# An attention and expert kernel: the start-up of the attention phase in another order, and two tensor-engine waits at other places in every pass

## The reference

```python
xn = layernorm(x)
# attention on xn, 16 heads of 64, latent width 128
h = layernorm(xn) * ln_scale + ln_bias
c_q, c_kv = h @ w_down_q.T, h @ w_down_kv.T
q, k, v = c_q @ w_up_q.T, c_kv @ w_up_k.T, c_kv @ w_up_v.T     # then rotary turns on q and k
s = softmax(q k^T / 8) v @ w_out.T + xn
# mixture of 8 experts on xn, the two best per token, each with a capacity
g = silu(experts(xn) + xn)
out = x + s * g
```

## Time and profile before

| | |
|---|---|
| median of 3 runs | 3656.07 us (3655.32 to 3656.79) |
| the profiled execution | 3655.32 us, its span 3653.8 us |
| PE busy | 3599.4 us, 99% of the span |
| DVE busy | 3195.1 us, 87% |
| ACT busy | 2759.1 us, 76% |
| POOL busy | 1199.8 us, 33% |
| granted TensorE clock | 0.998 of full speed over the span |

### The profile page before, as it was taken

How to read it: one execution, slowest core, us unless ns; L and a number is a source line. 1 busy time by engine, 2 the same in 40 slices (tenths; PEclk the granted TensorE clock), 3 DMA queues, 4 the chain that set the end, 5 groups by cost and what they waited for, 6 DMA issues and landing times. The chain is left out here.

```text
span 3653.8 us, 77190 instructions
## 1 busy us (share of the span) xinstructions
PE 3599.4 (99%) x24217; PEld 2364.0 (65%) x24217; DVE 3195.1 (87%) x4341; ACT 2759.1 (76%) x4016; POOL 1199.8 (33%) x1178
## 2 busy tenths in 40 slices
PE   7999999999999999999999999999999999999999
PEld 5754554545544554545554555454699999999999
DVE  8889999999999999999999999999777777777799
ACT  5778888888878888888888888888766666666665
POOL 2212222222222222222222222232366666666400
PEclk9999999999999999999999999999999999999999
DMA  7985767676666666666667676765666666666798
GB/s 257 358 283 142 185 156 186 157 185 161 180 160 176 170 174 169 171 171 166 177 165 181 160 186 156 184 162 136 193 222 215 217 223 216 214 224 216 235 369 274
DMA packets 378436, 724.74 MB, mean 198 GB/s; under 512 B 105277, under 2 KB 253886, under 8 KB 342272
## 3 DMA queue, kind: packets, MB, share of 16 engines
q0 software_dynamic: 83504, 340.66, 36.2%
q1 hardware_dynamic: 294864, 383.23, 31.8%
HBM read 453.60 MB, written 138.81 MB: 162 GB/s over the span
## 5 line engine op out<-in xcount | busy, mean ns | idle before, releaser
L1180 ACT ACTIVATE at_ex<-at_st 128x1024 f32<-128x1024 f32 x1024 | 1048.8, 1025 | 138.3 <-PE at_st L1327 132.8
L1383 PE MATMUL at_pv<-at_ex,at_v 128*64 128x512 f32 x4096 | 991.6, 605 | 0.0
L1037 DVE TENSOR_REDUCE at_mx<-at_fr 128x1 fp32r<-128x512 f32 x1024 | 705.9, 689 | 202.5 <-PE at_fr L1393 169.6
L1204 ACT ACTIVATE at_fr<-at_fr 128x512 f32<-128x512 f32 x1024 | 603.4, 589 | 243.0 <-PE at_fr L1393 229.7
L1383 PEld LDWEIGHTS at_pv<-at_ex,at_v 128*64 128x64 f32 x4096 | 248.3, 136 | 471.1 <-issue 462.2
L1050 DVE TENSOR_TENSOR at_sum<-at_sum,at_ex 128x1024 f32<-128x1024 f32 x448 | 545.3, 1217 | 3.7 <-ACT at_ex L1180 3.4
L1393 PE MATMUL at_fr<-at_kfar,at_qh 64*128 64x512 f32 x1024 | 459.7, 449 | 5.9 <-DVE at_mx L1037 4.5
L1390 PE MATMUL at_fr<-at_kdif,at_qh 64*128 64x512 f32 x1024 | 461.4, 451 | 1.8 <-DVE at_mx L1037 0.9
L1327 PE MATMUL at_st<-at_qh,at_kh 64*128 64x512 f32 x2048 | 452.8, 392 | 3.8 <-DMA at_top<-at_mneg 3.7
L1390 PEld LDWEIGHTS at_fr<-at_kdif,at_qh 64*128 64x128 f32 x1024 | 187.7, 183 | 413.7 <-issue 356.9
L1327 PE MATMUL at_st<-at_ql,at_kh 64*128 64x512 f32 x2048 | 452.0, 391 | 0.0
(11 more groups left out here) (213 smaller groups left out, 6359.4 us busy)
## 6 DMA issues: line engine op xcount, KB each, us to landing
at_cq<-scr_c SPq DMA_DIRECT2D x62, 1024.0 KB, 6.1
at_ck<-scr_c SPq DMA_DIRECT2D x62, 1024.0 KB, 5.2
at_sum<-at_sum POOLq DMA_DIRECT2D x95, 512.0 KB, 6.0
scr_v<-pj_v SPq DMA_DIRECT2D x64, 512.0 KB, 6.8
at_v<-scr_v SPq DMA_DIRECT2D x64, 512.0 KB, 6.6
mid_rec<-scr_rec SPq DMA_DIRECT2D x256, 128.0 KB, 5.1
scr_o<-mid_oT SPq DMA_DIRECT2D x64, 512.0 KB, 3.0
at_rotq<-at_swpq POOLq DMA_DIRECT2D x126, 256.0 KB, 4.6
```

The lines of the kernel that those rows point to most:

```text
L1037: e.reduce_max(mx[k // QB][:, h * QB + k % QB:h * QB + k % QB + 1], fr[h][:, :], AX.X).then_inc(s_tr[h], 1)
L1180: e.activation(ex[k][:, :, :], st[u % 2][:, :, :], ACT.Exp, scale=SCALE).then_inc(s_exp, 1)
L1204: e.activation(fr[h][:, :], fr[h][:, :], ACT.Relu).then_inc(s_pos[h], 1)
L1383: mm = e.matmul(pv[n][rows[h], :], v[i.u][:, kt, rows[h]], ex[kt][:, h, :], start=(kt == 0), stop=(kt == KT - 1))
```

## The change

It has four pieces.

1. **SP's prologue.** The loads of pair 2's weights (`load_w(At(0, 2), x)`) and the move of the first maxima go from behind the second value store to behind all value stores, behind the wait for their completion, and behind `load_v` of pair 0.
2. **PE's prologue and the routing.** The second routing product goes to the other half of `st[0]` in place of `pv[0]`. All four routing matmul groups are issued at k = 3 and 4, the two projections of pair 2 after them, the second one after k = 5. PE now waits for the rank ahead of body 0, where it waited for the totals. DVE does one more piece of `choice` (three, not two) before body 0. ACT's copies follow the projections.
3. **ACT's bodies.** Copies of the second projection halves (`proj_copy(two, K, 1)` and `proj_copy(three, Q, 1)`) move from the beginning of steps 4 and 0 to the end of the step before.
4. **PE's bodies.** `side_ready(g)`, which matters at g = 1 and g = 4, moves from behind `scores(2g+1)` to between `scores(2g)` and `scores(2g+1)`. A wait of `side(4)` for a copy joins it.

```diff
-        route_at = [st[0][:, 0, :], pv[0][:, :]]
+        route_at = [st[0][:, n, :] for n in range(2)]
...
                     if t == 1:
                         pj_compressed()
-                        e.wait_ge(s_made, 4)
-                        for x in (Q, K):
-                            e.wait_ge(s_pr, projected(At(0, 0), x, 1))
-                            load_w(At(0, 2), x)
-                            e.sem_inc(s_ld[x][0], 16)
-                e.wait_ge(s_init, 2)
-                max_rows(At(0, 0), 0)
                 pj["stored"](e)
                 pj["values_stored"](e)
                 load_v(At(0, 0))
+                for x in (Q, K):
+                    e.wait_ge(s_pr, projected(At(0, 0), x, 1))
+                    load_w(At(0, 2), x)
+                    e.sem_inc(s_ld[x][0], 16)
+                e.wait_ge(s_init, 2)
+                max_rows(At(0, 0), 0)
...
-                for _ in range(2):
+                for _ in range(3):
                     next(choice)
...
-                    if g == 0 and prev and ahead >= 2:
-                        proj_copy(two, Q, 1, pv[0])
-                    if g == 4 and ahead >= 2:
-                        proj_copy(two, K, 1, pv[1])
...
-                    if g == 1 and ahead >= 2:
-                        proj_copy(two, K, 0, pv[1])
+                    if g in (1, 3) and ahead >= 2:
+                        proj_copy(two, K, g // 2, pv[1])
...
-                    if g == 5 and ahead >= 3:
-                        proj_copy(three, Q, 0, pv[0])
+                    if g in (5, 7) and ahead >= 3:
+                        proj_copy(three, Q, (g - 5) // 2, pv[0])
...
-                    if k == 3:
-                        e.wait_ge(s_raw[K], 4)
-                        project(third, Q, 0, pv[1])
+                    if k in (3, 4):
+                        next(choice)
                     if k == 4:
-                        next(choice)
                         e.wait_ge(s_raw[K], 3)
                         e.wait_ge(s_init, 3)
                         turn_maxima(first, 0)
-                    if k == 5:
-                        e.wait_ge(s_neg, 1)
-                        next(choice)
                     step_y(first, k)
...
-                    if k == 3:
+                    if k in (3, 4):
                         next(choice)
                     if k == 4:
-                        e.wait_ge(s_raw[Q], 5)
-                        project(third, Q, 1, pv[1])
-                    if k == 5:
-                        next(choice)
+                        e.wait_ge(s_raw[K], 4)
+                        project(third, Q, 0, pv[1])
+                e.wait_ge(s_raw[Q], 5)
+                project(third, Q, 1, pv[1])
                 e.wait_ge(s_init, 2)
-                rt["counted"](e)
+                rt["ranked"](e)
...
                         scores(i, 2 * g)
+                        side_ready(g)
                         scores(i, 2 * g + 1)
-                    side_ready(g)
```

More of the change, by code:

```diff
@@ L704, in vector @@
             e.tensor_scalar(keep["widx"][:, :], who[:, :], float(P), part[:, 0:1], ALU.mult, ALU.add).then_inc(s_done, 1)
-        def counted(e):
-            e.wait_ge(s_v, 1)
         def ranked(e):
@@ L716, in done @@
             e.wait_ge(s_done, 3)
-        return {"vector": vector, "scalar": scalar, "tensor": tensor, "counted": counted, "ranked": ranked, "spread": spread, "done": done}
+        return {"vector": vector, "scalar": scalar, "tensor": tensor, "ranked": ranked, "spread": spread, "done": done}
 def attend_parts(nc, ctx, below, bridge, io, scr, keep, pj, rt):
@@ L1248, in prologue @@
                     if k == 4:
-                        proj_copy(third, Q, 0, pv[1])
                         negate(first, 0)
                     if k == 5:
-                        proj_copy(third, Q, 1, pv[1])
+                        proj_copy(third, Q, 0, pv[1])
                     gain(first, k, 1, s_y)
@@ L1257, in prologue @@
                         pj_value(2 * k + 3)
+                proj_copy(third, Q, 1, pv[1])
                 pj["values_stored"](e)
@@ L1512, in bank_free @@
                         e.wait_ge(s_neg, i.n(2, 1))
-                        if not prev:
-                            rt["ranked"](e)
                     elif prev:
@@ L1538, in side_ready @@
                             e.wait_ge(s_one[n], prev.n(16, 16))
+                        if ahead >= 2:
+                            e.wait_ge(s_raw[K], two.n(2, 2))
+                        else:
+                            e.wait_ge(s_neg, i.n(2, 2))
                 def side(g):
@@ L1550, in side @@
                     if g == 4 and prev:
[L1551 to L1554, removed]
                         denominators(prev)
```

## The result

The changed kernel takes 3683.36 us (median of 4, 3681.42 to 3687.47), the kernel before 3656.43 us (median of 4): 1.0075 times the time before, 95% interval 1.0057 to 1.0092. I had forecast 3680 us, 1.0065. A repetition in another session gave 3682.45 us, 1.0062 (1.0045 to 1.0079) of a kernel before that took 3660.38 there.

The account below looks back on a forecast made before the run. PE, busy 2098.21 of 2100 us, bounds the steady bodies; DVE paces body 0. Span 3653.8 + 12.8 (bodies) + 11.0 (prologue) = 3677.6, with 1.5 around it 3679.1, median 0.75 higher: 3680 us; 8-in-10 range 3667 to 3690.

Parts of the forecast that it names:

- The g = 1 wait: PE's bodies: `scores(3)` waits for ACT's copy, net 0.21 us in each of 61 bodies, 12.8 us in all.
- The wait at g = 4: PE's bodies, before `scores(9)`: its additions and copy come while PE still has four score pairs; cost taken as nothing.
- `step_y`'s own small stall: PE's step 1: 0.11 us against an undisturbed start, expected to disappear because `gain` is by then long over.
- ACT's copies at zero: ACT's bodies: the moved copies, about 0.6 us each, fit barely into gaps before steps 4 and 0; no cost.
- The prologue: Parts 1 and 2: 10.5 for later body 0, 1.7 for the clock, 1.2 back: +11.0 us, bounds +6 to +17.
- The landing of the weights: SP's prologue: pair 2's load goes out behind `v` and lands at about 243.5; PE stands from about 236.7, 6.8 us.
- The chain through DVE: Prologue, from weights landing through projection, maxima, scan, sizes and rank to PE entering body 0: 7.3 us.
- the start of body 0: End of the prologue: PE enters body 0 at 250.8 where it entered at 240.26, +10.5 us.
- one slow stretch: Prologue: the stall for the weights drops PE's clock to 1.2 GHz once, +1.7 us.
- The bound for two drops: Prologue: the clock also falls at the wait for the rank, 3.3 us long; 3.4 us in all.
- DVE's relief of body 0: Body 0: the rank no longer lies inside it, where DVE sets the pace; -1.2 us.
- The rule on the clock: Prologue: lower clock is default, only activity lifts it; slow stretches after both stalls would make the sum 1.7 us higher.

Follow-up runs that it names:

- e1: Changed kernel with the step-1 and step-4 waits put back behind `scores(2g+1)`, all else still changed: 3671.19 us, 1.0039 times the kernel before.
- e2: Kernel before with only the waits of steps 1 and 4 moved between `scores(2g)` and `scores(2g+1)`: 3673.15 us, 1.0044.
- e6: Changed kernel with ACT's `high(one, Q)` moved from the end of step 0 to step 1, behind `out_copy` and the first `gain`: 3663.32 us, 1.0019.
- e5: Kernel before with ACT's `high(one, Q)` moved from the end of step 0 to step 1, behind `out_copy` and the first `gain`: 3647.86 us, 0.9979.
- e7: Kernel before with only ACT's copies of the second projection halves moved to the end of the step before: 3655.72 us, 0.9999.
- e3: Changed kernel with SP's weight loads of pair 2 back behind the second value store; routing order and wait for the rank stay changed: 3677.35 us, 1.0058.
- e9: Changed kernel with 32 matmuls added ahead of the projection that waits for the weights and 14 ahead of PE's wait for the rank: 3681.29 us, 1.0063.
- e4: Changed kernel with 32 matmuls of 128x512 added on PE directly ahead of the projection that waits for the weights: 3685.74 us, 1.0081.
- e8: Kernel before with only SP's prologue changed: pair 2's weights and first maxima go out behind `load_v`; PE keeps its old order: 3674.07 us, 1.0054.

## Why the prediction was right

**The g = 1 wait (12.8 us forecast).** Shown: e1 and e2 isolate the two moved waits together, and e6 shows that it is the end of the copy that PE waits for. The wait at g = 4 was put at nothing, and between 300 and 2530 us no idle of PE above 0.15 us stands behind it in any trace. The common distance grew by 0.25 us, not 0.21. Outside the loop it grew by less, 0.16 us (36.93 to 37.09 from body 2 to 3), and there the way from the copy's end to PE's next weight load is shorter too: 0.05 us in pair 2, where the copy ends at 335.38, and 0.11 us in the loop, 1412.37 to 1412.48 (below). I had taken 0.06 us from `step_y`. 61 x 0.25 would be 15.3 us, and the ten traces give 14.9; that the profiled execution has 12.9, so close to 12.8, is chance. In the execution before PE had lost more time in single bodies (a few took 37.1 to 37.7 us) than in the one after: four times before, once after, it waited at `scores(8)` for the DMA of the row maxima to `top`, 1.7 us in all against 0.2. The rest of these bodies I did not trace further.

**`step_y`'s own small stall is given back.** Right, 0.39 us in place of 0.49. e5 takes it away in the kernel before too, and its 61 bodies are 7.2 us shorter.

**ACT's copies at zero.** Right (e7).

**The prologue (11.0 us forecast, 13.0 measured).** The landing of the weights was put at 243.5 on the old scale; 241.23 + 2.5 is 243.8. The chain through DVE from the projection to body 0 was put at 7.3 us; e3, at full clock up to there, has 242.36 - 235.06 = 7.30. Without the clock, which cost 0.9 us ahead of body 0, the start of body 0 moved by 11.7 - 0.9 = 10.8 us, forecast 10.5. The term that was mis-sized is the clock: I took +1.7 us for one slow stretch, from the earlier trace rows, and e9 measures 3.0. One stretch it was, but it went from 238 to 254, through both stalls and the score pairs of step 0 of body 0. The bound for two drops, 3.4 us, holds it. DVE's relief of body 0 was put at 1.2 us. From the start of body 0 to ACT's copy in body 1 the kernel before takes 287.23 - 240.26 = 46.97 us and e9, at full clock, 294.79 - 248.59 = 46.20. Of these 0.8 us e7 has 0.5 by ACT's moved copies alone, so that some 0.3 us are left for DVE. So the prologue is 10.8 + 3.0 - 0.8 = 13.0. That is 2.0 us more than forecast, and the bodies are 2.1 more; the median came out 3.4 us above 3680. Each part of this split rests on one or two executions.

**The rule on the clock.** The Trainium skill, "TensorE: Matmul & The Clock Gate", Part 1, has the lower clock as the default that activity lifts. Its fall agrees here, and for both stalls: with the first covered (e4) or gone (e3), the second, 3.5 us long, is followed by slow score pairs. The prediction drew from the rule that the sum would be 1.7 us higher, 3.4 for the clock. That is near the 3.0 measured, but partly by luck: in the changed kernel the clock did not come back between the stalls, so that there was one long stretch and not two short ones. How it comes back is less simple than one row suggested: see the last section.

## What to carry to other kernels

A wait that costs nothing where it stands has a distance to its event, and moving it forward by less than a microsecond can use that up in every pass: read, for each moved wait, when its event comes and when the engine would get there, and count the passes. Where an engine is saturated, look not only at what it waits for but at what stands ahead of that on the other engine: moving one ACT instruction of 1 us behind the copy that PE needs gained 8 us, and healed the moved wait as well. A load put behind the completion of stores inherits their whole landing time, here 6.9 us, and a stall of PE at such a place is paid a second time in its clock: 3.48 us of waiting for the rank cost 5.7 us (e3).

## What was not expected of the hardware

The clock came back later than the earlier trace rows had led me to think. There the slow stretch ended within the 24 matmuls; three microseconds behind the earlier trace rows the kernel before has

```profile
32.00:33.00 1.00, 1.00 (x6) 0.84 (x5) 1.00 (x4) 0.64 (x1) 0.00 (x0) 1.00 0.02 8
```

In e8, PE was busy 12.00 of 12.00 us after its stall and the granted clock was 0.50 all the way (the row above), with the same kinds of matmul as ever, projections, maxima steps and routing products in turns. In e9, with 32 and 14 matmuls of 128x512 back to back, it stayed at full level through both waits, and body 0 started fast:

```profile
234.00:249.00 15.00, 13.75 (x62) 10.43 (x62) 6.38 (x14) 2.61 (x5) 0.64 (x1) 1.00 0.55 146
```

What in the mix decides was not tried.

The time from the end of ACT's copy to PE's next weight load, at the moved wait, is 0.05 us in the bodies outside the loop and 0.11 us inside it. PEld's timeline in pair 2, and in a body of the loop:

```profile
335.43 0.18 PEld L1319 LDWEIGHTS at_st<-at_qh,at_kh 64*128 64x128 f32 x2 [0.48 <-ACT mid_osb L1205]
...
1412.48 0.19 PEld L1319 LDWEIGHTS at_st<-at_qh,at_kh 64*128 64x128 f32 x2 [0.55 <-issue]
```

That the semaphore values are computed in registers there is the difference in the code; that this is the cause was not tested. It can't be the whole of it: `step_y` of the kernel before waits in the same loop, and it started 0.06 us behind its `gain`.
